# One of eight FFN chunks per batch taken from the exp phase into the next round's score phase

## The reference

```python
x = x + attn(layernorm(x), Wq, Wk, Wv, Wo, gate)   # 16 heads of 16; softmax attention and a
                                                   # linear attention (elu + 1), mixed by sigmoid(gate)
x = x + ffn(layernorm(x), W1, W2, W3)

def ffn(x, W1, W2, W3):                            # D = 256, H = 1024
    up_gate = jnp.einsum('bsd,hd->bsh', x, W1)
    up_lin = jnp.einsum('bsd,hd->bsh', x, W3)
    hidden = fwht(jax.nn.silu(up_gate) * up_lin)   # the kernel folds fwht into W2
    return jnp.einsum('bsh,dh->bsd', hidden, W2)
```

## Time and profile before

| | us |
|---|---|
| median of 3 runs | 236.3 |
| their range | 234.07 to 237.19 |
| the profiled execution's own time | 234.01 |
| its span, first to last instruction | 232.1 |

### The profile page before, as it was taken

The page is one execution under the profiler, slowest core; times in us unless marked ns, Lnnn a source line. Parts: engine busy times, 40 slices in busy tenths (PEclk is TensorE's granted clock), DMA queues, the critical chain, the costliest instruction groups (busy, mean ns, idle before and its releaser), DMA issues.

```text
span 232.1 us, 4131 instructions
## 1 busy us (share of the span) xinstructions
PE 198.8 (86%) x1492; PEld 173.0 (75%) x1492; DVE 160.3 (69%) x337; ACT 96.9 (42%) x196; POOL 92.2 (40%) x81
## 2 busy tenths in 40 slices
PE   0585899869997599999998999999689999859894
PEld 0474789745595599977977989778589977649892
DVE  6766786485679977198899774679988364954432
ACT  3373112258730335687003346870124668022331
POOL 8612998744053572336013932520112133012232
PEclk9999999997999799999997999999999999999999
DMA  6977800000450000032400000325000100000101
GB/s 198 385 265 170 232 8 0 0 6 18 127 138 0 0 0 8 3 87 80 113 0 3 0 7 3 90 82 154 0 3 6 45 3 1 0 4 0 47 3 45
DMA packets 12817, 13.55 MB, mean 58 GB/s; under 512 B 1436, under 2 KB 12156, under 8 KB 12796
## 3 DMA queue, kind: packets, MB, share of 16 engines
q1 hardware_dynamic: 11468, 12.10, 17.5%
q10 hardware_dynamic: 1328, 1.19, 2.0%
HBM read 5.71 MB, written 1.05 MB: 29 GB/s over the span
## 4 chain that ended last, share of the span: by engine, by line
PE 49%; issue 24%; DVE 11%; POOL 8%; ACT 3%; DMA 1%; ACTq 1%; POOLq 1%; DVEq 0%
PE score_bank L925 6%; PE exp_bank L943 5%; POOL hid_lo L550 4%; PE exp_bank L1034 4%; PE score_bank L1034 4%; PE down_bank L1056 3%; DVE rowmax_pad L657 3%; PE pv_bank L960 3%; PE pv_bank L1073 3%; PE down_bank L1073 3%; PE misc_bank L993 2%; POOL wide_raw L556 2%; PE exp_bank L1038 2%; PE score_bank L1038 2%; PE down_bank L1060 2%
## 5 line engine op out<-in xcount | busy, mean ns | idle before, releaser
L657 DVE TENSOR_REDUCE rowmax_pad<-score_bank 128x2 f32<-128x512 f32 x64 | 43.1, 686 | 11.6 <-PE score_bank L925 11.5
L550 POOL TENSOR_TENSOR hid_lo<-wide_raw,hid_hi 128x256 fp32r<-128x256 f32 x32 | 23.8, 745 | 66.6 <-ACT hid_hi L409 66.6
L376 ACT ACTIVATE prob<-exp_bank 128x512 f32<-128x512 f32 x64 | 36.8, 601 | 15.5 <-PE exp_bank L943 15.1
L925 PE MATMUL score_bank<-k_stack,q_stack 128*128 128x256 f32 x128 | 32.2, 341 | 9.5 <-DVE rowmax_pad L657 8.1
L925 PEld LDWEIGHTS score_bank<-k_stack,q_stack 128*128 128x128 f32 x128 | 22.1, 200 | 13.0 <-DVE rowmax_pad L657 7.6
L943 PE MATMUL exp_bank<-q_stack,k_stack 128*128 128x256 f32 x128 | 26.2, 305 | 2.4 <-DMA q_stack<-nmT_lo 1.3
L943 PEld LDWEIGHTS exp_bank<-q_stack,k_stack 128*128 128x128 f32 x128 | 18.9, 193 | 9.8 <-ACT prob L376 5.4
L765 DVE SCALAR_TENSOR_TENSOR wide_raw<-wide_raw,score_bank 128x256 f32<-128x256 f32 x16 | 6.7, 419 | 22.3 <-ACT wide_raw L403 22.3
L1012 PE MATMUL pv_bank<-wo,att 128*128 128x256 f32 x64 | 16.7, 385 | 2.7 <-DVE att L750 2.7
L1056 PE MATMUL down_bank<-w_hi,hid_hi 128*128 128x256 f32 x64 | 17.5, 296 | 1.4 <-ACT hid_hi L409 1.4
L388 ACT ACTIVATE xs<-pv_bank 128x512 f32<-128x512 f32 x4 | 2.4, 597 | 36.0 <-DVE stats L621 36.0
(11 more groups left out here) (130 smaller groups left out, 519.2 us busy)
## 6 DMA issues: line engine op xcount, KB each, us to landing
q_stack<-part_hi SPq DMA_DIRECT2D x16, 128.0 KB
k_stack<-part_hi SPq DMA_DIRECT2D x14, 128.0 KB
xs<-in_x SPq DMA_DIRECT2D x4, 256.0 KB, 3.3
wide_raw<-in_w1T SPq DMA_DIRECT2D x1, 1024.0 KB, 8.4
wide_raw<-in_w3T SPq DMA_DIRECT2D x1, 1024.0 KB, 10.5
prob<-in_w2T SPq DMA_DIRECT2D x1, 1024.0 KB, 12.8
q_stack<-part_lo SPq DMA_DIRECT2D x8, 128.0 KB
out_y<-xs SPq DMA_DIRECT2D x8, 128.0 KB, 1.8
```

The costliest lines, as they stand in the source:

```text
L376: act.activation(prob[:, h % 8], exp_bank[h % 2][:], ACT.Exp, scale=SCALE).then_inc(prob_s, 1)
L550: pool.tensor_tensor(hid_lo[:, n % 3, :], ffn_work[n % 3], hid_hi[:, n % 3, :].bitcast(F32), ALU.subtract).then_inc(hid_lo_s, 1)
L657: dve.tensor_reduce(rowmax[:, h, :], score_bank[h % 2][:], AX.X, ALU.max).then_inc(rowmax_s, 1)
L925: mm = pe.matmul(bank[:, tt, :], q_stack[:, h, tt * P:tt * P + P], k_stack[:, h, :], start=True, stop=True)
```

## The change

For batches 0, 1 and 2, chunk 6 is treated as chunk 7 already is: all of its steps are taken out of round r's exp phase and put into the score phase of the round after. Batch 3's chunk 6 keeps its place. On TensorE its two ups come at h = 2 and h = 3, each as the last thing of that head, behind `project_out` steps 1 and 2, and its down at h = 8 behind the layernorm's transposes. On ScalarE its `ffn_tanh` becomes the round's first instruction, ahead of `evac_x2`, and its `split_hid` comes right behind `evac_x2`. On VectorE its `ffn_gate` comes at h = 4, ahead of the layernorm statistics. On GpSimd its `hid_low` becomes the round's first instruction, ahead of `rope_sums` and `ln_power`. Its bank becomes `exp_bank[0]`. The `split_hid` of chunk 5, which went along with chunk 6's tanh, stays at h = 12 of the exp phase.

```diff
         def chunk_bank(n):
-            return (exp_bank if n % FC in (7, 0, 1, 2) else score_bank)[n % 2]
+            return (exp_bank if n % FC in (6, 7, 0, 1, 2) else score_bank)[n % 2]
...
 # scalar
             for r in range(0, NB + 1):
+                if has(r - 2):
+                    ffn_tanh(chunk(r - 2, 6))
                 if has(r - 1):
                     evac_x2(r - 1)
+                if has(r - 2):
+                    split_hid(chunk(r - 2, 6))
                 if has(r + 1):
                     split_parts(r + 1, 0)
...
-                    if h in (2, 6, 12):
+                    if h in (2, 6) or h == 12 and r == NB:
                         ffn_step(chunk(r - 1, {2: 4, 6: 5, 12: 6}[h]))
+                    elif h == 12 and has(r - 1):
+                        split_hid(chunk(r - 1, 5))
...
-                    if h == 15 and has(r - 1):
-                        if r == NB:
-                            ffn_tanh(chunk(r - 1, 7))
+                    if h == 15 and r == NB:
+                        ffn_tanh(chunk(r - 1, 7))
                         split_hid(chunk(r - 1, 6))
 # gpsimd
             for r in range(0, NB + 1):
+                hid_low(chunk(r - 2, 6))
                 if has(r + 1):
                     rope_sums(r + 1, 0)
...
-                for c in range(2, FC if r == NB else FC - 1):
+                for c in range(2, FC if r == NB else FC - 2):
                     hid_low(chunk(r - 1, c))
 # vector
+                    if h == 4:
+                        ffn_gate(chunk(r - 2, 6))
                     if h == 4 and has(r - 1):
                         ln_statistics(LN[(2, r - 1)])
...
-                ffn_gate(chunk(r - 1, 6))
+                if r == NB:
+                    ffn_gate(chunk(r - 1, 6))
                 if has(r):
                     combine(r, 0)
 # tensor
+                    if h in (2, 3):
+                        ffn_up(chunk(r - 2, 6), h - 2)
                     if h in (6, 7):
                         ffn_up(chunk(r - 2, 7), h - 6)
-                    if h == 10:
-                        ffn_down(chunk(r - 2, 7))
+                    if h in (8, 10):
+                        ffn_down(chunk(r - 2, h // 2 + 2))
...
-                    if h in UP_IN_EXP:
+                    if h in UP_IN_EXP and (r == NB or UP_IN_EXP[h][0] < 6):
                         c, m = UP_IN_EXP[h]
                         ffn_up(chunk(r - 1, c), m)
...
-                ffn_down(chunk(r - 1, 6))
+            ffn_down(chunk(NB - 1, 6))
             ffn_down(chunk(NB - 1, 7))
```

## The result

The changed kernel takes 243.94 us (median of 4 runs, 243.22 to 245.02), the kernel before 235.19 us (233.88 to 237.19). The ratio is 1.0398, with a 95% interval of 1.0345 to 1.0452; it is taken over the fast runs of each kernel alone, so it is not quite the quotient of the two medians. I had forecast 236.8 us and a range of 232.0 to 240.2: wrong, and outside the range.

The account below looks back on a forecast made before the run. TensorE was taken to bound the exp phases, VectorE's row maxima the score phases. Rounds 2, 3 and 4 gave +1.9, -0.35 and -1.1 us, sum +0.45, taken as +0.5: median 236.3 becomes 236.8 us, range 232.0 to 240.2.

Parts of the forecast that it names:

- Statistics to normalisation: Second layernorm: GpSimd's hid_low delays the power; 4.5 us in round 2 (was 2.65), 3.2 in rounds 3 and 4 (was 2.1).
- Rival (a): Score phases: GpSimd's new wait holds nobody up; rounds 2 to 4 give 0, -1.5, -2.25 us, so 232.6 us; chance 0.22.
- The clock: Round 2, behind the transposes: the extra 0.7 us down fits, as the slow-clock stretch there moves into the wait.
- rival (b): Half-speed stretches behind the transposes, up to 1.7 us each, 5.1 in rounds 2 to 4 together: 241.9 us; chance 0.18.
- fell where TensorE had to wait anyhow: Round 2, kernel before: most of the 1.7 us lost to the slow clock lay in TensorE's waits.
- The exp phase: Rounds 1 to 3: TensorE leaves it 1.7 to 1.8 us earlier, 1.0 from the ups and 0.7 from the down.
- The bound of 0.7: Lower bound, in us, of each exp phase's gain, if ScalarE's exponentials give nothing; the upper bound was 2.1.
- The way to the statistics: From exp phase to second layernorm's statistics: round 2's start as before, round 3's 1.5 us earlier, round 4's chain about 2.25 ahead.
- The mixing: VectorE's combine, freed from waiting behind chunk 6's gate, comes 1.4 us earlier in round 1 and 2.0 in round 2.
- the gate, which I had called hidden: Round 4: VectorE idled 1.22 us before the statistics, so the gate costs nothing; 0.8 us if that cover were gone.
- L747 beside `hid_lo`: VectorE's 512-column L747 no longer runs beside GpSimd's hid_lo: from 1.15 to about 0.7 us, counted as 0.45.
- Sum: Whole kernel: rounds 2, 3 and 4 give 1.9 - 0.35 - 1.1 = +0.45 us, taken as +0.5.

Follow-up runs that it names:

- version 5: Kernel before, chunk 6 untouched, plus an unread ScalarE copy and a GpSimd subtraction waiting for it at its queue's head, rounds 2 to 4: 243.81 us, ratio 1.0341.
- version 6: version 5 plus needless repeats of chunk 7's up matmuls in TensorE's gaps before heads 7 and 8: 239.16 us, ratio 1.0202.
- version 10: Kernel before with only chunk 6's down moved, from the exp phase's end to h = 6 of the next round: 233.98 us, ratio 0.9993.
- version 7: Changed kernel with chunk 6's hid_low behind the power, plus 6 needless matmuls at h = 8 and 11 of exp phases 1 to 3: 236.74 us, ratio 1.0106.
- version 2: Changed kernel with chunk 6's down at h = 7, in TensorE's wait, instead of h = 8: 240.15 us, ratio 1.0193.

## Why the prediction was wrong

**Statistics to normalisation: right.** I forecast 1.9 us for round 2 and 1.15 each for rounds 3 and 4, 4.2 in all. The traces give 1.82, 1.19 and 1.19, which is 4.2. Versions 5 and 6 show the cause alone. Rival (a), that the wait would hold nobody up, is refuted by them.

**The clock: the step that failed most.** "TensorE's own extra down of 0.7 fits behind the transposes, since I take the slow-clock stretch that lay there (below) to move into the wait" gave the stage behind the normalisation 0; it cost 5.0 us. The stretch didn't fall in the wait: it began 0.6 us after the normalisation, in the last part of TensorE's gap, lasted twice as long (6.8 us), and new ones came in rounds 3 and 4. By round that stage grew by 2.5, 1.4 and 1.0 us. That is rival (b), to which I had given a chance of 0.18; that its total of 5.1 us came so near is partly luck, as it had 1.7 us in each round. Against it I had held that rounds 3 and 4 waited before at full clock. That was no evidence for longer waits, which my own working had just added: in round 3 TensorE's gaps before heads 7 and 8 went from 0.60 and 0.52 us to 1.21 and 1.73. First the rows before, then those after the change:

```profile
166.56 0.50 PE L925 MATMUL score_bank<-k_stack,q_stack 128*128 128x256 f32 x2 [0.60 <-DVE rowmax_pad L657]
...
168.28 0.47 PE L925 MATMUL score_bank<-k_stack,q_stack 128*128 128x256 f32 x2 [0.52 <-DVE rowmax_pad L657]
```

```profile
171.57 0.50 PE L934 MATMUL score_bank<-k_stack,q_stack 128*128 128x256 f32 x2 [1.21 <-DVE rowmax_pad L663]
...
174.50 0.76 PE L934 MATMUL score_bank<-k_stack,q_stack 128*128 128x256 f32 x2 [1.73 <-DVE rowmax_pad L663]
```

The Trainium skill, "TensorE: Matmul & The Clock Gate", section "What's actually happening", which I had cited for the fall after idling, pointed the right way. The trace agrees with it here: round 2's fall came in the gap of 2.94 us. I weighed it too lightly.

My other premise, that the stretch of the kernel before "fell where TensorE had to wait anyhow", was right, but the earlier trace rows don't show it (TensorE was busy 3.97 of those 4 us). Version 10 does: without that stretch round 2's stage behind the normalisation is as long (16.3 us).

**The exp phase: mis-sized.** I forecast 1.7 to 1.8 us a round, 1.0 of it from the ups. Measured: 1.06, 0.71 and 0.83. The down alone gives 0.77, 0.75 and 0.80 of it (version 10), so the ups gave 0.3 in round 1 and nothing in the other two. The bound of 0.7, "if the exponentials give nothing", was nearly the truth. Rows of the changed kernel's exp phase in round 2 show it:

```profile
153.25 0.50 PE L952 MATMUL exp_bank<-q_stack,k_stack 128*128 128x256 f32 x2 [0.57 <-ACT prob L376]
...
155.88 0.50 PE L952 MATMUL exp_bank<-q_stack,k_stack 128*128 128x256 f32 x2 [0.46 <-ACT prob L376]
...
158.79 1.09 ACT L376 ACTIVATE prob<-exp_bank 128x512 f32<-128x512 f32 x2 [0.71 <-PE exp_bank L952]
```

TensorE waits for the exponential of two heads ago, and after the product with v ScalarE waits for TensorE. With two exp banks they take turns, and the ups had filled TensorE's turns of waiting (version 7 puts matmuls back there, at no cost in two of three rounds). A gapless TensorE looked like a TensorE that sets the time; it was one whose waits were filled.

**The way to the statistics.** I forecast that they would come 0, 1.5 and 2.25 us earlier, counted from the exp phase's start, in rounds 2, 3 and 4. They came 0.76 later, 0.32 and 0.59 earlier. Of the 3.6 us that are missing, 2.7 are the exp phase above (about 5.3 forecast, 2.6 had). The rest, 0.9 us, lies nearly all in round 4. The mixing was indeed 1.5 to 1.6 us earlier (I had 1.4 and 2.0), but in rounds 3 and 4 the two ups stand ahead of the last output projection, which then waited for no one: TensorE's order had become the bound. And in round 4 the gate, which I had called hidden, was not. It waited for its tanh, and the statistics came about 0.4 us after the last projection's end (before: at once):

```profile
210.35 1.03 PE L1021 MATMUL pv_bank<-wo,att 128*128 128x256 f32 x4
...
210.97 0.42 DVE L771 SCALAR_TENSOR_TENSOR wide_raw<-wide_raw,exp_bank 128x256 f32<-128x256 f32 x1 [1.52 <-ACT wide_raw L403]
...
211.77 0.76 DVE L627 BATCH_NORM_STATS2 stats<-pv_bank 128x6 f32<-128x256 f32 x2
```

**L747 beside `hid_lo`:** right, and worth little. Rows of the changed kernel, end of round 2's exp phase:

```profile
157.67 0.73 POOL L555 TENSOR_TENSOR hid_lo<-wide_raw,hid_hi 128x256 fp32r<-128x256 f32 x1 [1.53 <-ACT hid_hi L409]
157.87 0.56 DVE L739 TENSOR_TENSOR ginv<-inv,gate 128x16 f32<-128x16 f32 x1
...
159.21 0.69 DVE L753 TENSOR_TENSOR att<-att,narrow_raw 128x512 f32<-128x512 f32 x1
```

The multiplication fell from 1.15 us to 0.69. But with the mixing earlier, `hid_lo` of chunk 5 now meets L739, which took 0.17 us at its place before and takes 0.56: 0.46 won, 0.39 given back.

**Sum.** Forecast +0.45 us; measured on the span +9.3: 4.2 right, 5.0 for the clock put at nothing, and 3.75 of gains expected up to the statistics of which 0.15 came. The remaining 0.3 lies ahead of round 1's exp phase and is no part of the change. What stays open is why the clock fell in just these places and for how long: the half-speed stretches in round 1 and around 51 to 55 us are 3.4 or 6.8 us long from one version to another with the same work, and executions of one kernel differ as well (the mean clock of the kernel before lay between 0.956 and 0.985).

## What to carry to other kernels

When a step moves, place it in each engine's queue behind the instructions that others wait for: a small operation at the head of an idle engine's queue, waiting for a late input, cost about 3.4% here, half of it through the clock behind the wait (versions 5 and 6). Treat TensorE work between two waits as possibly free filler; before counting its removal as a gain, ask what TensorE waits for once it is gone. And where a forecast lengthens gaps in front of a gapless stretch of matmuls, count the clock as a likely term with its price from the trace, not as a remote one.

## What the runs showed of the hardware that I had not expected

Eighteen needless matmuls a round made the kernel 5 us quicker (243.94 to 238.8 us), with the normalisation as late as before (11.0 us), because the granted clock behind the gaps stayed at 1.00. In version 2, 0.7 us of real work moved into round 2's gap left 2.22 us of the 2.94 idle, and the clock stayed at 1.00 there too. And one half-speed stretch could be twice as long as another: 6.8 us in round 2 of the changed kernel, in which TensorE was busy all the time from 128 us on, against 3.4 us in the kernel before. The gaps' lengths alone don't tell which: in round 3 the gaps of 1.21 and 1.73 us were followed by 3.4 us at half speed, and those of 0.61 and 1.74 us in version 5 by 6.8.
